# Shorter early tile lists, nine leading tiles and later row places in a fused graph layer and expert layer

## The reference

```python
# x: 128 graphs x 128 nodes x 128 features
x = x + gnn(layernorm(x), adj)      # eps*x + adj@x, @W1 + b1, RMS norm, SiLU, @W2 + b2
x = x + moe_block(layernorm(x))
# moe_block(u): logits = u @ gate_w + gate_b; top 2 of 16 experts, softmax of the two logits
#   expert e: relu(u @ w1[e] + b1[e]) @ w2[e] + b2[e]        (128 -> 256 -> 128)
#   y = u + weighted sum of the two experts' outputs; layernorm(y) * gamma + beta
```

## Time and profile before

| what | value |
|---|---|
| median of 3 runs | 851.79 us (847.35 to 851.98) |
| the profiled execution's own time | 845.29 us |
| its span in the trace | 843.5 us |
| PE, DVE, ACT, POOL busy | 88%, 74%, 63%, 61% |
| HBM traffic | 99.67 MB read, 65.55 MB written |

### The profile page before, as it was taken

How to read it: one execution, slowest core, us unless ns; L and a number is a source line. 1 busy time by engine, 2 the same in 40 slices (tenths; PEclk the granted TensorE clock), 3 DMA queues, 4 the chain that set the end, 5 groups by cost and what they waited for, 6 DMA issues and landing times.

```text
span 843.5 us, 18675 instructions
## 1 busy us (share of the span) xinstructions
PE 740.7 (88%) x4709; PEld 570.2 (68%) x4710; DVE 624.7 (74%) x2289; ACT 529.3 (63%) x1123; POOL 517.6 (61%) x540
## 2 busy tenths in 40 slices
PE   4999999999999999995279999999999999999910
PEld 3677877788777777874157777777677777777610
DVE  2589999999999998886666777666666666666574
ACT  2599999999999999985223333454444444444442
POOL 3004777777677767777540027777767776777774
PEclk9999999999999999997589999999999999999965
DMA  5445555555545443221667778999999999999842
GB/s 160 133 147 172 170 171 171 187 191 191 186 173 181 162 169 120 74 82 56 185 161 207 203 213 250 267 263 275 270 272 280 273 261 287 271 279 271 254 134 94
DMA packets 141243, 165.84 MB, mean 197 GB/s; under 512 B 18803, under 2 KB 94723, under 8 KB 141190
## 3 DMA queue, kind: packets, MB, share of 16 engines
q1 hardware_dynamic: 122614, 129.87, 50.3%
q0 software_dynamic: 16384, 34.11, 14.2%
q10 hardware_dynamic: 2192, 1.31, 0.6%
HBM read 99.67 MB, written 65.55 MB: 196 GB/s over the span
## 4 chain that ended last, share of the span: by engine, by line
SPq 22%; POOL 12%; issue 10%; DVE 4%; DMA 4%; PE 1%; ACT 1%; POOLq 1%; DVEq 0%; ACTq 0%
POOL work L492 9%; SPq L378 7%; SPq L386 5%; SPq L393 4%; SPq L395 4%; DMA results<-tout 3%; POOL rows L492 3%; ACT rows L745 1%; POOL dispatched L473 1%; SPq L419 1%; DMA dispatched<-rows,slot_i 1%; DVE tout L1188 1%; POOLq L481 0%; PE bank L586 0%; DMA work<-results,place 0%
## 5 line engine op out<-in xcount | busy, mean ns | idle before, releaser
L473 POOL DMA_INDIRECT dispatched<-rows,slot_i x256 | 258.9, 1011 | 166.4 <-issue 159.5
L492 POOL DMA_INDIRECT work<-results,place x184 | 181.6, 987 | 125.9 <-DVE tout L1188 71.3
L805 ACT ACTIVATE hid<-bank,wts 128x256 f32<-128x256 f32 x286 | 119.9, 470 | 220.2 <-PE bank L672 220.2
L1188 DVE SCALAR_TENSOR_TENSOR tout<-bank,gate,tin 128x128 f32<-128x128 f32 x286 | 87.2, 346 | 129.8 <-DMA results<-tout 100.4
L672 PE MATMUL bank<-tut,wts 128*128 128x256 f32 x572 | 152.9, 390 | 23.0 <-DVE tut L1171 18.8
L687 PE MATMUL bank<-wts,hid 128*128 128x128 f32 x1144 | 165.7, 288 | 0.0
L687 PEld LDWEIGHTS bank<-wts,hid 128*128 128x128 f32 x1144 | 138.5, 191 | 17.1
L524 PEld LDWEIGHTS bank<-w_sb,work 128*128 128x128 f32 x1024 | 123.2, 194 | 17.6 <-issue 14.6
L524 PE MATMUL bank<-w_sb,work 128*128 128x128 f32 x1024 | 126.4, 278 | 1.6 <-ACT work L784 1.6
L672 PEld LDWEIGHTS bank<-tut,wts 128*128 128x128 f32 x572 | 98.5, 192 | 39.4 <-DVE tut L1171 24.0
L518 PE MATMUL bank<-agg,w_sb 128*128 128x512 f32 x256 | 124.7, 610 | 0.0
(11 more groups left out here) (188 smaller groups left out, 1045.8 us busy)
## 6 DMA issues: line engine op xcount, KB each, us to landing
wts<-in_w_exp SPq DMA_DIRECT2D x143, 257.0 KB, 4.1
tin<-dispatched SPq DMA_DIRECT2D x143, 132.0 KB
results<-tout SPq DMA_DIRECT2D x26, 704.0 KB, 5.5
results<-tout SPq DMA_DIRECT2D x143, 128.0 KB
xs<-in_x SPq DMA_DIRECT2D x32, 256.0 KB, 3.4
adj_sb<-in_adj_t SPq DMA_DIRECT2D x32, 256.0 KB
rms_b<-r_row SPq DMA_DIRECT2D x32, 256.0 KB, 3.5
out<-agg SPq DMA_DIRECT2D x32, 256.0 KB, 4.7
```

Source lines behind the costliest of these rows:

```text
L473: nc.gpsimd.indirect_dma_start(dispatched, bass.IndirectOffsetOnAxis(slot_i[:, k, n:n + 1], 0), rows[:, k, n // TOPK, n % TOPK, :], None). ...
L492: nc.gpsimd.indirect_dma_start(moe_of(g)[:, n // TOPK, n % TOPK, :], None, results, bass.IndirectOffsetOnAxis(place[:, g, n:n + 1], 0)).th ...
L805: last = nc.scalar.activation(hid[:, n % 2, c, :], hid_ps[n % 2][:, c * TILE:(c + 1) * TILE], ACT.Relu, bias=wts[:, k, F + FC * D + c:F + ...
L1188: last = nc.vector.scalar_tensor_tensor(out=tout[:, k, a, :], in0=exp_ps[n % 2][:, a * D:(a + 1) * D], scalar=gate[:, n % 2, a:a + 1], in1 ...
```

## The change

Three things change together.

- The list ends become 2, 4, 6, 9, 12, 15, 18, 21, 25 and 29 groups, from 3, 4, 7, 8, 11, 15, 19, 23, 27 and 29. `MIX_FROM`, which follows from the ends and `FIRST`, becomes 42 from 39.
- `FIRST` becomes 9, from 6. SyncE's waits for all scatters and for the padding rows stood ahead of the first store and of the loads of tile 7 (the seventh tile); now they stand inside the step that stores the fourth tile and loads the tenth, between the two.
- The calls of `places` move: the first from ahead of the first tile to tile step 0, together with two small tables, the others to tile steps 6, 38, 52, 64, 76, 88 and 100.

```diff
-FIRST = 6
+FIRST = 9
 FULL_AT = 29
-SEGS = (3, 4, 7, 8, 11, 15, 19, 23, 27, FULL_AT)
+SEGS = (2, 4, 6, 9, 12, 15, 18, 21, 25, FULL_AT)
+PLACES_AT = (6, 38, 52, 64, 76, 88, 100)
...
-            def tile_step(i, t, entries=table):
+            def tile_step(i, t, entries=table, ahead=None):
...
                         sp.dma_start(results[bass.ds(d, TILE), :].rearrange("(a p) d -> p a d", p=P), tout[:, k])\
                             .then_inc(t_kept[k], 16)
+                    if ahead is not None:
+                        ahead()
                     if loads:
...
-            for n in range(RING2, FIRST):
-                tile_step(None, n - 4, entries=first_table)
-            sp.wait_ge(padded, 16 * (E + 1))
             sp.wait_ge(table_done, 1)
             sp.wait_ge(kept_done, 1)
-            for k in range(RING):
-                sp.wait_ge(scattered[k], 16 * GB * TOPK * len(range(k, NG, RING)))
+
+            def all_dispatched():
+                sp.wait_ge(padded, 16 * (E + 1))
+                for k in range(RING):
+                    sp.wait_ge(scattered[k], 16 * GB * TOPK * len(range(k, NG, RING)))
+
+            for n in range(RING2, FIRST):
+                tile_step(None, n - 4)
+            tile_step(None, FIRST - 4, ahead=all_dispatched)
...
-            pipeline(sp, tile_step, FIRST - 4, lead, turns, MIX_FROM, RING2)
+            pipeline(sp, tile_step, FIRST - 3, lead, turns, MIX_FROM, RING2)
...
-            link(nc.vector.tensor_reduce(need_f[:], upto_t[0:1, NS, :], axis=AX.X, op=ALU.add))
-            nc.vector.tensor_scalar(need[:, NS - 2:], need_f[:], float(LAG), None, ALU.add).then_inc(need_done, 1)
-            dve.wait_ge(rows_done, 2)
-            nc.vector.tensor_copy(table[:, RING2:, 2], misc_ps[0:1, 0:NT]).then_inc(kept_done, 1)
...
-            places(None, 0)
+
+            def late_tables():
+                link(nc.vector.tensor_reduce(need_f[:], upto_t[0:1, NS, :], axis=AX.X, op=ALU.add))
+                nc.vector.tensor_scalar(need[:, NS - 2:], need_f[:], float(LAG), None, ALU.add).then_inc(need_done, 1)
+                dve.wait_ge(rows_done, 2)
+                nc.vector.tensor_copy(table[:, RING2:, 2], misc_ps[0:1, 0:NT]).then_inc(kept_done, 1)
+                places(None, 0)
...
-                if i is None and t in (0, 3):
-                    places(None, 1 + t // 3)
-                if i is not None and t == 7 + RING2 - 1:
-                    places(i, 3)
+                if i is None and t == 0:
+                    late_tables()
+                if i is None and t in PLACES_AT:
+                    places(None, 1 + PLACES_AT.index(t))
```

More of the change, by code:

```diff
@@ L914, in first_tiles @@
                 past = q_ps[:, 0:FULL_AT * E].rearrange("p (s e) -> p s e", e=E)
[L915 to L920, removed]
+                for first, step, n, at in ((0, 2, 3, 0), (6, 3, 5, 3), (21, 4, 2, 8)):
+                    link(nc.vector.tensor_scalar(
+                        nt_i[:, 0, at:at + n],
+                        past[:, first:first + step * n].rearrange("p (b c) e -> p b c e", c=step)[:, :, step - 1],
+                        float(TILE - 1), None, ALU.add))
                 link(nc.vector.tensor_scalar(nt_i[:, 0, 10:11], past[:, FULL_AT - 1:FULL_AT], 0.0, None, ALU.add))
```

## The result

The changed kernel takes 854.99 us (median of 20 runs, 850.13 to 860.61), the kernel before in the same rounds 851.12 us (20 runs, 847.35 to 855.07). The ratio is 1.0052, with a 95% interval of 1.0036 to 1.0068: it is slower by half a per cent, where 0.6% faster was forecast.

A forecast was written before the change was run, and what follows sets the result against it. The end is set by the latest list release plus the gathers behind it: group 25 at 756.0 plus 82.7 gives 838.7 against 843.5, 4.8 us faster, a median of 847.0 us, range 841.5 to 855.5.

The forecast's parts named there:

- T127: End of the 127th tile, which releases group 25's gathers: forecast at 755.2 us, against 764.4 before.
- the list's price at unchanged tile times: The list at 127 tiles now holds back group 25, not 27: end at 847.9, slower by 4.4 us.
- Up to T4: Start of the tile stage to the fourth tile's end: 437.3 against 441.7, 4.4 us earlier.
- T4 to T20: Tiles 5 to 20: one call of places instead of two, 1.5 us saved, 40.5 us against 42.0.
- T20 to T58: Next 38 tiles at 2.42 us plus two calls at 1.5: tile 58 ends at 572.8, against 581.6.
- T58 to T127: Saturated part, taken as DMA-limited: 182.8 us as before, less 1.2 for list waits, plus 0.8 for late calls.
- the wait takes the call in: Last four calls, during `out` stores: VectorE's existing store wait absorbs them, leaving 0.2 us each, 0.8 in all.
- Rival (a): Saturated DMA, late calls and earlier gathers eat the 8.8 us lead; wholly lost, median 856.2; chance 0.15.
- break-even: The end of tile 127 at which the change neither gains nor loses: 760.0 us.
- Rival (b): Late calls and those at steps 38 and 52 cost nothing, waits give back more: median 842.2; chance 0.15.

The follow-up runs named there:

- F: The kernel before with nine leading tiles and their early stores alone: ratio 0.9955.
- L and F: The changed kernel with the calls of places put back where they were, so new list ends and nine leading tiles: ratio 1.0024.
- threes: The kernel before with nine leading tiles and list ends 3, 6, 9, ..., 27, 29, calls of places where they were: ratio 0.9929.
- F and P: The changed kernel with the old list ends, so nine leading tiles and moved calls of places: ratio 1.0001.
- the doubled kernel: The changed kernel with the six late calls of places repeating their first instruction three times: ratio 1.0301 on the second chip, whose runs count.
- the spread kernel: The changed kernel with each call of places but the first spread over four tile steps, one instruction in each: ratio 0.9980.
- P alone: The kernel before with only the calls of places and the two small tables moved: ratio 1.0090.
- the second trace of the kernel before: The kernel before, unchanged, profiled once more: 849.39 us.

## Why the prediction was wrong

**What bounds the kernel: right.** The end is the release of the last list that binds and the gathers behind it. Group 25 started 0.8 after T127 in the changed kernel, and the list's price at unchanged tile times, 4.4 us, was measured four times as 0.47% to 0.69% of 851, 4.0 to 5.9 us. The time from group 25 to the end was 84.4 for 82.7.

**The forecast of T127: wrong by 15.6 us in the traces** (770.8 for 755.2). By stretches:

- Up to T4, 1.9 of it. The first `tut` copy came at 425.10, not at 423.6: the tile stage starts 1.3 later in this trace (first loads at 405.08, not 403.80), which is chance, since the traces range from 402.9 to 406.1; and TensorE's transposes at the lower clock end 0.9 after VectorE is free. Tile 1 didn't gain 1.9 but nothing (432.0), about 1 if the later start is taken off. The early stores did what was said: tile 3 has no store wait, and the moved wait for the scatters cost nothing.
- T4 to T20: 40.5 for 40.5, in part by luck. A call taken out here was to save 1.5; F, L and F, and threes have two calls here and take 41.1 to 41.2, F and P and the doubled kernel have one and take 41.5 and 41.8.
- **T20 to T58, 5.5 (100.5 for 95.0). The first step that failed:** a pace of 2.42 for each tile without a call, and 1.5 more for each early call. Without any block that makes 92.0; the four kernels with spread calls take 97.8 to 98.3, and the six traces with three early calls 96.1 to 99.0. So three calls there cost nothing in sum, and taking them out gave nothing back. The 2.42 was read over 13 tiles between two other stretches and isn't kept; without a call VectorE waits for stores instead. The two calls at steps 38 and 52, priced at 3.0, cost 2.7 by the spread kernel.
- **T58 to T127, 8.2 (190.6 for 182.4). The second step that failed:** "the wait takes the call in", at 0.2 for each of four late calls. VectorE's wait for a store is not free time for TensorE. While VectorE waits there, the next tile's `tut` has already been copied and TensorE works on; a call in front of that copy stops TensorE. With the calls spread the stretch takes 184.8, so the four blocks cost 5.8, not 0.8 (3.3 by the same pair with the old lists, 190.7 and 187.4). The other 3.2 are the pace: 181.6 were forecast without a call, and the ten traces without a late block take 182.4 to 187.9. What makes the tiles slower here when they come earlier was not isolated.

**The sign.** Against the kernel before 4.8 us of gain were forecast; the ratio 1.0052 is 4.4 us of loss, 9.2 apart. The forecast held 3.8 us for the six late calls, so without them it stood for a gain of 8.6. The kernel with the calls spread gains 1.7: 6.9 of the 9.2 us are a lead that never came, from T20 on above all. The block costs 6.1, not 3.8: the other 2.3. The missing lead turns the sign by itself: with the calls at the price forecast the kernel would still be 2.1 us slower than before. The block's price alone would not: with the lead as forecast and the block at 6.1 it would be 2.5 us faster. (Each ratio is known to about 2 us.) What the change can be spared without touching its lists is the block: 0.9980 instead of 1.0052.

The parts don't add: P alone costs 0.90%, on F 0.46%, on L and F 0.28%. The end follows T127 with the new lists and the release of group 19 with the old ones (715.1 in P, 703.6 in F and P). P's calls stand in another quarter of a turn, and its low stretches last 23.9 us from 525 to T127 against 13.7 in F and P and in the changed kernel; which of these makes it so much dearer I have not separated.

**The rivals.** Rival (a), time given back so that break-even is missed, came true and had 0.15. Of its mechanism the late calls are shown. Saturated DMA engines are neither shown nor refuted: in the changed kernel they are less busy in the tile stage (0.92 in 580 to 771) than with spread calls (0.94), so they don't account for the calls' part; but in F, L and F and threes, with no late call, a lead of 4.1 to 5.3 us at T58 over the second trace of the kernel before is down to less than 1 at T127, which is what (a) said; with spread calls it is kept in two kernels of four. Rival (b) took the late calls as free; it was the forecast's own error, taken further. That an earlier first gather is worth nothing by itself, which follows from the forecast's own bound, holds: 10 us of it change nothing (841.90 and 841.98).

**The range** ended at 855.5 and holds the median; the direction was wrong, and that the median lies inside is no merit of the sum. A late call was bounded by 0 and 1.5. Six calls in one piece cost 6.1 and 5.8 us by the medians, 1.0 each; by the traces between T36 and T127 9.0 (248.4 - 239.4) and 6.8 (249.7 - 242.9), of which the first holds a changed kernel 3.3 us above its median.

## What to carry to other kernels

A wait of an engine is not room for work in front of the instruction on which another engine depends: ask what the other engine has left to do for the length of the block. Cut side work into pieces no longer than the gap that the consumer can bridge, and spread it over steps (here six calls of 2.4 us in one piece cost 6 us more than the same calls in pieces of at most 0.7 us). Don't carry a pace read over a few undisturbed tiles to a whole stage: take it from a long stretch, and take the price of a disturbance from stretches with and without it. Where a queue of transfers follows lists, the last list that binds sets the end: make the lists equally long before making the first one short.

## What was unexpected of the hardware

TensorE's granted clock fell from 2.4 to 1.2 GHz for 3.4 us in the midst of the tile stage, between 1 us before TensorE resumed and 2 us after, when it stood still for 1.8 to 4.0 us behind a call (533, 666 and 700 in the changed kernel, all six in the doubled one), and the same four matmuls then took 2.03 in place of 1.03. In the doubled run this came behind all six calls and lasted 6.8 us four times, and 13 us of extra VectorE work became 21 us. The length of a single stop doesn't decide it. In the changed kernel three of six stops had no fall (the three shorter ones, 0.98, 1.41 and 1.47 us); in F and P a stop of 1.27 had one (528.8) and a stop of 2.72 had none (666.8). Twice it came without a call (644.9 in the run with the lists alone; 740.9 in the changed kernel, where TensorE had waited 1.40 for a load and 0.82 for a copy). How much of the calls' cost is the clock's and how much the standstill's own was not separated. An estimate of the most that the clock can have cost: the four low stretches of the changed kernel last 13.7 us, in which TensorE at half its clock loses at most 6.8 of the 9.0 us by which T36 to T127 is longer than with spread calls.

The Trainium skill ("TensorE: Matmul & The Clock Gate", section "Part 1: The HAM clock gate") describes a gate that sets TensorE's clock by how busy the engine has lately been. The traces agree with that much: TensorE stood still ahead of the low stretches behind calls. No run here shows the condition.
